# Layer 0 of the next pass is moved into layers 1 to 3 of this pass

## The chip, the cores and the metric

The kernel runs on one core of a Trainium2 chip. The metric is the device time of one execution in microseconds (us). A sample is an image of 128 channels by 32 by 32 pixels in float32; 16 samples go through the kernel in one execution.

## What is computed

Four residual layers run one after the other, each as `x = x + layer(group_norm(x))`, with 32 groups of 4 channels:

```
layer 0: offsets, mask = conv3x3(x -> 3 channels); bilinear sampling of x at the
         moved points, times the mask; depthwise 3x3; 1x1 (128 x 128)
layer 1: avg_pool3(x); conv3x3 -> 18 offsets + 9 masks; each of 9 taps is sampled
         bilinearly at its moved point; 3x3 convolution of the samples (128 x 128)
layer 2: conv3x3 (128 x 128) with weights made from weight and r_matrix
layer 3: 1x1 in; two directions (rows, then columns) of: depthwise 7-tap, 1x1 to 5
         kernels per head, tanh, weighted sum of 5 taps; two gates; 1x1 out
```

## The kernel before

One pass handles two samples, s = 0 and s = 1; eight passes make the 16. Seven of them are turns of a hardware loop (`one_pass(i, True)`), the last is written out (`one_pass(i, False)`). Channels lie on the 128 partitions, so an image is a tile of 128 x 1024. Each engine has its own program, written out by hand, and runs it in the order in which it is written; semaphores (`x_ready`, `n_blk` and so on) are all that ties the engines together. There is no scheduler.

In program order a pass of TensorE does this:

1. `near0` for both samples: the sampling of layer 0 in 8 tiles each. For a tile TensorE transposes two strips (L520) and two products of the hat functions (L526) and multiplies them (L535); VectorE makes the products (L1205) and copies the strips from PSUM (`block_copy`, L1116), ScalarE copies the transposed products (`G`) and at the end the sampled image `img`.
2. The depthwise convolution and the 1x1 of layer 0 in one: `w0[k]` is the 1x1 weight times tap k, and TensorE adds 4 (s = 0) or 7 (s = 1) taps (L644), while VectorE adds up the other 5 or 2 taps (`DW_TAPS`, L1223 to L1227), which go through one more matmul (L651). A tap is two matmuls, one for each half h of the image. VectorE then adds the residual (L1232), takes the statistics (`stats`, L1042 to L1046) and, with a small matmul for the mean over each group (`group_mean`) and a power on GpSimd, makes the scale and the bias of the normalisation (`affine`, L1054 to L1065); ScalarE applies them (`normalise`, L823); VectorE makes the 3x3 box sums (`pool3`, four instructions, L1177 to L1183).
3. Layer 1, s = 0: `offset_parts` (L456), `offsets` (L466), `doubles`, `far` (a count of offsets that reach too far; `load_flag` and a branch follow on each engine), `blocks` (transposes of the image, L551). VectorE makes the hat functions (L1315 to L1327), then in `near` the products (L1338) and transposes (L1349) of 8 tiles, with the box sums of s = 1 in between; TensorE samples (L580) and ScalarE copies.
4. The convolution `w1` of s = 0 (L482), with the offsets and blocks of s = 1 hooked in between its matmuls (`between`, a dictionary from (half, tap) to work); then `near` and `w1` of s = 1.
5. `w2` of both samples (layer 2), then the last residual, statistics and normalisation.
6. Layer 3: `P_X2`, `P_U`, `P_XC`, `P_MEAN`, the kernels of the first direction (`P_KERN`), those of the second, `P_GATE`, `P_OUT`. VectorE does the depthwise taps (L1402, L1407) and the weighted sums (L1421 to L1449) of each direction. Hooked in between the two directions are the layer 0 preparations of the next pass: normalisation (ScalarE), `start_parts` (twice `offset_parts`), `start_offsets`, `start_far`, and on VectorE `start_hats`.

The PSUM tensors are `psO[0]`, and `psN`, four banks of which `psO[1]` is the first two and `psT` the last two; `ps[0]` and `ps[1]` hold small results.

## Time and profile before

| | us |
|---|---|
| median of 3 runs | 2032.02 (2031.22 to 2033.98) |
| the profiled execution | 2024.91 |
| its span, first to last instruction | 2023.0 |
| TensorE busy | 1685.6 (83%) |
| VectorE busy | 1242.0 (61%) |
| ScalarE busy | 597.7 (30%) |
| mean granted TensorE clock | 0.911 of full speed |

The profile was taken from one execution, which was 7.1 us shorter than the median. PE is TensorE, DVE is VectorE, ACT is ScalarE, POOL is GpSimd, PEld the weight loads of TensorE. A float32 matmul of 512 columns stands in the trace as two records; a transpose as one. Busy time of TensorE is modelled and counts overlaps of neighbours, so that it is somewhat too high.

### The profile page before, as it was taken

How to read it: one execution, taken by the hardware profiler on the slowest of the kernel's cores; microseconds unless marked ns; L12 is line 12 of the kernel's file. 1: busy time of each engine (PE TensorE's matmuls, PEld its weight loads, DVE VectorE, ACT ScalarE, POOL GpSimd, SP SyncE). 2: the span in 40 equal slices, each digit the busy share in tenths (PEclk: the TensorE clock that was granted, in tenths of full speed). 3: DMA queues.
4: the chain of work that ended last, by engine and by line, in shares of the span. 5: the costliest groups of instructions: out<-in, count | busy, mean ns of one | idle time of the engine just before them, and what ended most of it. 6: DMA issues, size and time to landing. Idle time of an engine off the chain costs nothing.

```text
span 2023.0 us, 23653 instructions
## 1 busy us (share of the span) xinstructions
PE 1685.6 (83%) x7748; PEld 905.4 (45%) x7748; DVE 1242.0 (61%) x2281; ACT 597.7 (30%) x986; POOL 78.8 (4%) x92
## 2 busy tenths in 40 slices
PE   4979878898788987889878888879878798797984
PEld 3555344543445434554345533555335553355431
DVE  5655676546775387753877439664496654865546
ACT  2232422324324142230513305133141322313221
POOL 1000000000000000000001000010000000000000
PEclk8999989898889988899888998889989899897997
DMA  2000000000000000000000000000000000000000
GB/s 97 22 1 1 1 23 22 1 1 1 23 22 1 0 1 23 22 1 0 1 23 22 2 0 1 33 12 1 0 1 33 12 1 0 1 22 1 1 0 21
DMA packets 7108, 22.80 MB, mean 11 GB/s; under 512 B 1233, under 2 KB 1937, under 8 KB 6929
## 3 DMA queue, kind: packets, MB, share of 16 engines
q1 hardware_dynamic: 6928, 20.58, 2.8%
q8 instruction: 92, 1.51, 0.3%
q14 instruction: 88, 0.71, 0.1%
HBM read 12.19 MB, written 8.39 MB: 10 GB/s over the span
## 4 chain that ended last, share of the span: by engine, by line
issue 73%; DVE 12%; PE 11%; POOL 2%; ACT 1%; DVEq 0%; POOLq 0%
PE psO L456 2%; DVE GQt L1349 2%; PE psO L482 1%; DVE GTs L1338 1%; POOL gst L407 1%; DVE samp L1407 1%; DVE hf L1315 1%; DVE img L1183 1%; DVE hf L1320 1%; PE ps L466 1%; POOL strip L415 1%; PE psN L482 1%; ACT xn L823 1%; DVE hf L1327 1%; DVE pool_v L1179 1%
## 5 line engine op out<-in xcount | busy, mean ns | idle before, releaser
L482 PE MATMUL psO<-samp,w 128*128 128x512 f32 x576 | 259.4, 596 | 10.1 <-ACT samp L801 10.1
L580 PE MATMUL psN<-GQt,xq 64*128 64x144 f32 x2048 | 188.2, 334 | 89.6 <-DVE GQt L1349 71.8
L823 ACT ACTIVATE xn<-x,gst 128x1024 f32<-128x1024 f32 x48 | 60.2, 1254 | 536.8 <-DVE gst L1065 536.8
L580 PEld LDWEIGHTS psN<-GQt,xq 64*128 64x128 f32 x2048 | 161.3, 215 | 122.6 <-issue 57.5
L801 ACT ACTIVATE samp<-psN 128x576 f32<-128x576 f32 x256 | 155.9, 649 | 161.5 <-PE psN L580 161.2
L482 PEld LDWEIGHTS psO<-samp,w 128*128 128x128 f32 x576 | 105.0, 190 | 118.9 <-issue 118.9
L482 PE MATMUL psN<-xn,w 128*128 128x512 f32 x288 | 131.5, 605 | 0.0
L482 PE MATMUL psO<-xn,w 128*128 128x512 f32 x288 | 129.8, 603 | 0.0
L801 ACT ACTIVATE xq<-psN 128x512 f32<-128x512 f32 x144 | 81.6, 598 | 85.4 <-PE psN L551 80.0
L1338 DVE TENSOR_TENSOR GTs<-hf 128x576 f32<-128x576 f32 x128 | 104.1, 823 | 3.4
L801 ACT ACTIVATE G<-psN 120x256 f32<-120x256 f32 x128 | 49.1, 384 | 187.9 <-PE psN L526 186.8
L644 PE MATMUL psN<-img,w 128*128 128x512 f32 x224 | 101.6, 604 | 0.0
L407 POOL TENSOR_TENSOR gst<-gst,neg_half 128x1 f32<-128x1 f32 x64 | 35.0, 548 | 1621.7 <-DVE gst L1059 1621.6
L1349 DVE STREAM_TRANSPOSE GQt<-GTs 128x576 f32<-128x576 f32 x128 | 96.9, 766 | 0.0
L551 PE MATMUL psN<-ident,strip 128*128 128x128 f32 x512 | 87.0, 333 | 0.0
L1054 DVE COPY gst<-ps 128x2 f32<-128x2 f32 x64 | 10.1, 158 | 124.6 <-PE ps L447 124.6
L743 PE MATMUL psN<-samp,kv_w 128*128 128x512 f32 x96 | 60.3, 761 | 30.9 <-DVE samp L1407 30.9
L551 PEld LDWEIGHTS psN<-ident,strip 128*128 128x128 f32 x512 | 73.2, 175 | 28.2 <-issue 20.5
L1250 DVE TENSOR_TENSOR om<-ps,offb 128x216 f32<-128x216 f32 x16 | 6.1, 383 | 129.2 <-PE ps L466 129.2
L482 PEld LDWEIGHTS psO<-xn,w 128*128 128x128 f32 x288 | 53.5, 188 | 68.6 <-issue 68.6
L1116 DVE COPY xblk<-psN 120x256 f32<-120x256 f32 x128 | 54.3, 424 | 46.5 <-PE psN L520 46.5
L482 PEld LDWEIGHTS psN<-xn,w 128*128 128x128 f32 x288 | 53.0, 188 | 64.8 <-issue 64.8
(162 smaller groups left out, 2656.5 us busy)
## 6 DMA issues: line engine op xcount, KB each, us to landing
xin<-in_x SPq DMA_DIRECT2D x16, 512.0 KB, 3.4
out<-yout SPq DMA_DIRECT2D x16, 512.0 KB, 2.7
w<-in_w SPq DMA_DIRECT2D x2, 576.0 KB, 5.4
samp<-in_r SPq DMA_DIRECT2D x1, 576.0 KB, 6.7
tab<-in_tab SPq DMA_DIRECT2D x1, 494.0 KB, 5.0
kh_w<-in_kh SPq DMA_DIRECT2D x1, 320.0 KB, 5.8
kv_w<-in_kv SPq DMA_DIRECT2D x1, 320.0 KB, 5.9
woT<-in_woT SPq DMA_DIRECT2D x1, 256.0 KB, 6.5
```

The lines of the kernel that those rows point to most:

```text
L407: nc.gpsimd.tensor_tensor(out=g[:, 18:19], in0=g[:, 17:18], in1=neg_half[:], op=ALU.pow).then_inc(rstd_ready.sem, 1)
L456: last = mm(dst[32 * g:32 * g + 32, h, :], w[:, k, :], window(src)(h, k), start=(k < 4), stop=(k >= K9 - 4), skip_group_check=True)
L482: last = mm(dst[:, h, :], wgt[:, k, :], rhs(h, k), start=(k == 0), stop=(k == K9 - 1))
L551: last = nc.tensor.transpose(psT[:, t % 2, C * n:C * n + C], block, ident[:])
L580: last = mm(pair(u)[:, g, :].rearrange("p (k r c) -> p k r c", k=K9, c=SW)[:, :, :, cols], xQ[rows, t, a, e, :], w[rows, e, :, :, cols], s ...
L644: mm(psO[s][:, h, :], w0[:, k - min(DW_TAPS), :], window(img[s])(h, k), start=(k == DW_TAPS[s]), stop=False)
L743: mm(product(m), lhsT, rhs[:, HALF * h:HALF * h + HALF], start=True, stop=True)\
L801: return nc.scalar.activation(out, in_, ACT.Copy)
L823: nc.scalar.activation(inner(xn[s]), src[:].rearrange("p (r c) -> p r c", c=W), ACT.Identity, bias=g[:, 20:21], scale=g[:, 19:20]).then_in ...
L1116: v_.tensor_copy(xblk[b][:].rearrange("p h c -> p (h c)"), psT[0:BLK, 1, 0:2 * C])\
L1338: v_.tensor_tensor(GQ[n % 2][:].rearrange("p (k a b) -> p k a b", a=QR, b=QB), hy[:, n].unsqueeze(3).broadcast_to((C, PAIRS * K9, QR, QB)) ...
L1349: v_.transpose(GQt[o % RING][:].rearrange("p e k r c -> p (e k r c)"), GQ[(n - 1) % 2][:])\
```

## The change

The kernel becomes a pipeline over passes. What a pass of the loop does now, in the order of TensorE:

- It begins with the taps of layer 0 of its own sample 1 (`conv0(i, 1, ...)`, 18 matmuls, all nine taps on TensorE), put around `offset_parts`, `offsets`, `doubles` and `far` of sample 0. VectorE adds the residual and takes the statistics of sample 1 (`second_sample(0)`) after the hat functions of sample 0 and before its products; `affine` follows at tile 2, the box sums at tiles 4 to 7.
- The statistics and normalisation of the next two inputs (S0, S1; into `img`) stand behind the sampling of s = 0, with their `group_mean` hooked into `w1` of s = 0.
- `offset_parts`, `offsets` and the far count of the next pass are hooked into `w1` of s = 1; VectorE makes their offsets and hat functions ahead of the residual of `w1` of s = 1.
- `near0` of the next pass is hooked into `w2`: tiles of sample 0 into the second half of `w2` of s = 0, those of sample 1 into `w2` of s = 1. Both `w2` now write `psO[1]`. The residual of layer 2 goes to `yout`.
- The taps of layer 0 of the next sample 0 (`conv0(i + 1, 0, ...)`, `fill`) stand in pieces ahead of and inside layer 3, and `kernels(0)` ahead of `P_U`. Between the two directions VectorE adds its residual and takes its statistics, `affine` comes after the depthwise taps of the second direction, and the box sums in two pairs ahead of the weighted sums of the two halves. ScalarE's `normalise` for it stands ahead of the tanh of the second direction.
- VectorE's own taps (`DW_TAPS`, L1223 to L1227) and the matmuls behind them (L651) go. Ahead of the loop stand `near0` of both samples of pass 0 and the taps, residual, statistics and box sums of its sample 0.

```diff
 NEAR0, NEAR = 2.0, 1.0
 EARLY, LATE = 6, 9
-DW_TAPS = (5, 2)
-DVE_STEPS = 114
-START_STEPS = 29
+DVE_STEPS = 138
+START_STEPS = 38
 
...
-        POOL_AT = (2, 3, 4, 5)
+        POOL_AT = (4, 5, 6, 7)
...
+        P_X2 = 1
+        P_KERN = P_X2 + 2
+        P_U = P_KERN + 2 * TAPS
+        P_XC = P_U + 2
+        P_MEAN = P_XC + 2
+        P_GATE = P_MEAN + 2 + 2 * TAPS
         P_OUT = P_GATE + 2
+
+        def p_kern(v, h):
+
+            return (P_MEAN + 2 if v else P_KERN) + TAPS * h
+
...
+        EVENTS = ("L1B", "S0", "S1", "L2A", "L2B", "L3A", "L3B", "L1A")
+        LAST = ("L1B", "L2A", "L2B", "L3A", "L3B")
+        FIRST = ("S0", "S1", "L1A")
...
+        def norm_ends(name):
+
+            k = SAMPLE[name]
+            if name in ("S0", "S1"):
+                return xin[k], img[k]
+            return (yout if name in ("L3A", "L3B") else x)[k], xn[k]
...
@@ TensorE @@
+            def layer0(j, i=None):
+
+
+                def conv2(n, between={}, halves=(0, 1)):
+                    if i is None:
+                        return
+                    if n:
+
+                        pe.wait_ge(added.sem, added.at(i, 5))
+                        pe.wait_ge(xn_ready.sem, xn_ready.at(i, nth("L2B", EVENTS)))
+                    conv(psO[1], w2, window(xn[n]), between, halves)
...
+                        conv2(0, {(1, k): lambda k=k: near0(j, 0, k - 2) for k in range(2, K9)}, (1,))
+                        near0(j, 0, TILES - 1)
+
+                        pe.wait_ge(added.sem, added.at(i, 4))
+                        near0(j, 0, TILES)
+                        hooks = {(0, 2): third_mean}
+                        for n, hk in enumerate(((0, 3), (0, 5), (0, 7), (1, 0), (1, 2), (1, 4), (1, 6), (1, 8))):
+                            hooks[hk] = lambda n=n: near0(j, 1, n)
+                        conv2(1, hooks)
+                        near0(j, 1, TILES)
...
+            def conv0(j, s, first, last):
+
+
+                if first == 0:
+
+                    pe.wait_ge(img_ready.sem, img_ready.at(j, s + 1))
+                    if s:
+                        pe.wait_ge(added.sem, added.at(j, 1))
+                for n in range(first, last):
+                    h, k = n // K9, n % K9
+                    ins = mm(psT[:, h, :], w0[:, k, :], window(img[s])(h, k), start=(k == 0), stop=(k == K9 - 1))
+                if last == 2 * K9:
+                    ins.then_inc(conv_ready.sem, 1)
+
...
+                conv0(i, 1, 0, 7)
...
+                pe.wait_ge(y_ready.sem, y_ready.at(i, 0))
                 pe.wait_ge(pooled_ready.sem, pooled_ready.at(i, 1))
                 offset_parts(2, img[0], w1off)
...
+                conv0(i, 1, 7, 10)
                 offsets(i, 2, 27)
+                conv0(i, 1, 10, 12)
                 doubles(i, 0)
+                conv0(i, 1, 12, 14)
                 far(i, 2)
-                blocks(i, 0, range(2, TILES))
+                conv0(i, 1, 14, 18)
+                blocks(i, 0, range(TILES))
...
-                        near(i, s)
+                        near(i, s, lambda t, s=s: group_mean(i, "L1B", order) if s == 0 and t == 0 else None)
...
+                        hooks = {(0, 2): lambda: blocks(i, 1, (2, 3)),
+                                 (0, 4): lambda: (second_offsets(), blocks(i, 1, (4, 5))),
+                                 (0, 6): lambda: doubles(i, 1),
+                                 (1, 0): lambda: far(i, 3), (1, 2): lambda: blocks(i, 1, (6, 7))}
+                        if more:
+                            hooks[0, 1] = lambda: group_mean(i, "S0", order)
+                            hooks[0, 3] = lambda: group_mean(i, "S1", order)
+                        conv(psO[0], w1, samples, hooks)
                     else:
+                        hooks = {(0, 5): lambda: group_mean(i, "L2A", order)}
+                        if more:
+                            hooks[0, 2] = lambda: next_parts(0)
+                            hooks[0, 7] = lambda: next_parts(1)
+                            hooks[1, 0] = next_offsets
+                            hooks[1, 4] = lambda: offsets(i + 1, 1, 3)
+                            hooks[1, 8] = lambda: start_far(i + 1)
 
                         pe.wait_ge(added.sem, added.at(i, 3))
-                        conv(psO[0], w1, samples, {(0, 4): lambda: group_mean(i, 4)})
-
-
-                pe.wait_ge(xn_ready.sem, xn_ready.at(i, 5))
-                conv(psO[1], w2, window(xn[0]), {(0, 6): lambda: group_mean(i, 5),
-                                                 **({(1, 4): lambda: start_means(i + 1, False)} if more else {})})
-                pe.wait_ge(xn_ready.sem, xn_ready.at(i, 6))
-                conv(psO[0], w2, window(xn[1]), {(0, 6): lambda: group_mean(i, block3_norm(0, more))})
-
-                group_mean(i, block3_norm(1, more))
-
-                pe.wait_ge(xn_ready.sem, xn_ready.at(i, 8))
+                        conv(psO[0], w1, samples, hooks)
...
+                conv(psO[1], w2, window(xn[0]), halves=(0,))
+                group_mean(i, "L2B", order)
+                if more:
+                    layer0(i + 1, i)
+                else:
+                    conv(psO[1], w2, window(xn[0]), halves=(1,))
+
+                    pe.wait_ge(added.sem, added.at(i, 5))
+                    pe.wait_ge(xn_ready.sem, xn_ready.at(i, nth("L2B", order)))
+                    conv(psO[1], w2, window(xn[1]), {(0, 6): lambda: group_mean(i, "L3A", order)})
+
...
+                fill(0, 4)
+                group_mean(i, "L3B", order)
+                fill(4, 7)
...
+                fill(7, 14)
+                kernels(0)
...
+                fill(14, 16)
...
+                fill(16, 18)
...
+                    group_mean(i, "L1A", order)
+                kernels(1)
...
@@ ScalarE @@
+                    if s and more:
+                        normalise(i, "S0", order)
+                    if s:
+                        blocks(i, s, range(4))
...
+                            if s == 0 and u == 5:
+                                normalise(i, "L1B", order)
...
+                if more:
+                    normalise(i, "S1", order)
+                    parts(i + 1, 0)
+                    wide(i + 1, 0, i, order)
+                normalise(i, "L2A", order)
+                if more:
+                    parts(i + 1, 1)
+                    wide(i + 1, 1, i, order)
+                    start_masks(i + 1)
+                normalise(i, "L2B", order)
+                if more:
+                    layer0(i + 1)
+                normalise(i, "L3A", order)
+                normalise(i, "L3B", order)
+
...
+                    normalise(i, "L1A", order)
+                kernels(1)
...
@@ VectorE @@
+            def residual0(j, s):
+
+                dve.wait_ge(conv_ready.sem, conv_ready.at(j, s + 1))
+                v_.tensor_tensor(x[s][:], psT.rearrange("p b c -> p (b c)"), xin[s][:], ALU.add)\
+                    .then_inc(added.sem, 1)
+                dve.wait_ge(added.sem, added.at(j, s + 1))
+
+            def residual2(i, s):
+
+                dve.wait_ge(conv_ready.sem, conv_ready.at(i, 5 + s))
+                if s == 0:
+
+                    dve.wait_ge(yout_free.sem, yout_free.at(i, 0))
+                v_.scalar_tensor_tensor(yout[s][:], psO[1][:].rearrange("p b c -> p (b c)"),
+                                        vec[:, V_B2:V_B2 + 1], x[s][:], ALU.add, ALU.add).then_inc(added.sem, 1)
...
+                with dve.Else():
+                    for s in range(2):
+                        for n in range(TILES + 1):
+                            if n < TILES:
+                                product(TILES * s + n)
+                            if n == TILES and s == 0 and i is not None:
+
+                                residual2(i, 0)
+                            if n:
+                                block_copy(j, TILES * s + n - 1, (n - 1) % 2)
+                        if s == 0:
+                            third_stats()
+                    dve.wait_ge(n_blk.sem, n_blk.at(j, 2 * TILES))
...
+                def second_sample(part):
 
                     if part == 0:
+                        residual0(i, 1)
+                        stats(own, "L1B", order)
+                    elif part == 1:
+                        affine(own, "L1B", order)
                     else:
+                        pool3(own, 1, part - 2, i, order)
...
+                            if s == 0 and n == 2:
+                                second_sample(1)
                             if s == 0 and n in POOL_AT:
 
-                                pool3(1, POOL_AT.index(n))
+                                second_sample(2 + POOL_AT.index(n))
...
+                    if s == 0 and more:
+                        for k in range(2):
+                            start_stats(own, i + 1, k, order)
+                        for k in range(2):
+                            affine(own, ("S0", "S1")[k], order)
                 for s in range(2):
+                    if s and more:
+                        start_offsets(own, i + 1)
+                        for k in range(2):
+                            start_hats(own, i + 1, k)
 
...
+                    if v and more:
+                        residual0(i + 1, 0)
+                        stats(own, "L1A", order)
...
-                    if more and v == 1:
-                        start_offsets(nxt)
+                    if v and more:
+                        affine(own, "L1A", order)
                     for h in range(2):
+                        if v and more:
+                            for part in range(2 * h, 2 * h + 2):
+                                pool3(own, 0, part, i, order)
 
```

## Rows read from the trace of the kernel before

**Rows 1.** The page, part 1: busy time and instructions of the whole span.

```profile
PE 1685.6 (83%) x7748; PEld 905.4 (45%) x7748; DVE 1242.0 (61%) x2281; ACT 597.7 (30%) x986; POOL 78.8 (4%) x92
```

**Rows 2.** Windows of the second pass: length, busy (count) of each engine, PEclk, DMA.

```profile
285.70:332.40 46.70, 41.23 (x183) 25.38 (x182) 30.11 (x55) 9.56 (x21) 0.55 (x1) 0.96 0.08 27
332.40:352.90 20.50, 14.72 (x92) 9.70 (x93) 14.04 (x27) 7.09 (x13) 2.66 (x2) 0.81 0.09 27
352.90:371.60 18.70, 13.06 (x128) 11.41 (x129) 14.54 (x17) 9.97 (x16) 2.39 (x1) 0.77 0.00 1
371.60:401.30 29.70, 28.40 (x126) 14.51 (x126) 10.40 (x17) 5.62 (x12) 0.00 (x0) 0.93 0.01 1
401.30:414.50 13.20, 10.38 (x129) 8.68 (x129) 12.17 (x18) 9.54 (x16) 0.00 (x0) 1.00 0.01 2
414.50:469.80 55.30, 48.89 (x120) 21.68 (x120) 17.55 (x53) 5.02 (x4) 3.28 (x6) 0.98 0.00 0
469.80:534.80 65.00, 54.12 (x192) 21.26 (x192) 55.17 (x99) 27.49 (x41) 0.00 (x0) 0.86 0.02 7
```

**Rows 3.** Timeline of TensorE, second pass: start us, length us, work [idle before <-releaser].

```profile
288.44 0.43 PE L520 MATMUL psN<-ident,strip 128*120 128x128 f32 x2 [2.64 <-issue]
...
308.91 7.30 PE L644 MATMUL psO<-img,w 128*128 128x512 f32 x16 [0.58 <-PE psN L535]
...
332.42 4.61 PE L456 MATMUL psO<-img,w1off 128*32 128x512 f32 x36 [0.24 <-DVE img L1183]
...
380.81 1.04 PE L551 MATMUL psN<-ident,strip 128*128 128x128 f32 x8
381.69 1.88 PE L482 MATMUL psO<-samp,w 128*128 128x512 f32 x4
383.41 1.86 PE L466 MATMUL ps<-tab,Gd 128*128 128x27 f32 x16
...
469.82 3.68 PE L734 MATMUL psO<-xn,win2T 128*64 128x512 f32 x8 [3.12 <-ACT xn L823]
```

**Rows 4.** Timeline of VectorE, second pass: residual, statistics, box sums, affine.

```profile
317.96 1.22 DVE L1232 TENSOR_TENSOR x<-psO,xin 128x1024 f32<-128x1024 f32 x1 [2.38 <-PE psO L651]
...
321.13 0.22 DVE L1046 SCALAR_TENSOR_TENSOR gst<-gst 128x1 f32<-128x1 f32 x1 [0.27 <-DVE gst L1044]
...
327.23 1.29 DVE L1177 TENSOR_TENSOR pool_v<-xn 128x1088 f32<-128x1088 f32 x1 [1.33 <-ACT xn L823]
...
331.14 1.23 DVE L1183 TENSOR_TENSOR img<-img,pool_v 128x1024 f32<-128x1024 f32 x1
...
338.21 0.16 DVE L1054 COPY gst<-ps 128x2 f32<-128x2 f32 x1 [2.78 <-PE ps L447]
...
339.67 0.21 DVE L1065 TENSOR_SCALAR gst<-gst 128x1 f32<-128x1 f32 x1
```

**Rows 5.** Timeline of VectorE around the first sampling of layer 1.

```profile
343.98 2.16 DVE L1315 TENSOR_TENSOR hf<-tab,om 128x288 f32<-128x288 f32 x4 [0.71 <-DVE flag L1108]
...
350.65 1.43 DVE L1338 TENSOR_TENSOR GTs<-hf 128x576 f32<-128x576 f32 x2
...
366.05 1.42 DVE L1349 STREAM_TRANSPOSE GQt<-GTs 128x576 f32<-128x576 f32 x2
```

**Rows 6.** Timeline of ScalarE inside layer 3.

```profile
480.42 2.39 ACT L823 ACTIVATE xn<-xin,gst 128x1024 f32<-128x1024 f32 x2
482.69 1.25 ACT L984 ACTIVATE samp<-psO,vec 128x512 f32<-128x512 f32 x2
```

**Rows 7.** Timeline of VectorE inside layer 3.

```profile
483.98 0.69 DVE L1439 SCALAR_TENSOR_TENSOR samp<-x2p,samp 128x512 f32<-128x512 f32 x1 [1.01 <-ACT samp L984]
...
491.79 0.69 DVE L1439 SCALAR_TENSOR_TENSOR samp<-x2p,samp 128x512 f32<-128x512 f32 x1 [1.37 <-ACT samp L984]
...
522.64 0.15 DVE L1108 CAST flag<-ps 128x1 int32<-128x1 f32 x1
...
525.63 0.43 DVE L1079 SCALAR_TENSOR_TENSOR hat<-hat,mk 128x256 f32<-128x256 f32 x1
```

563 lines of the change are left out of this document (266 added, 297 removed).

## The prediction

> **What bounds the kernel now.** I began with the page's busy shares: TensorE is busy 83% of the span, VectorE 61% [rows 1]. That average says little, so the second thing read was the windows of one pass, the second, cut where TensorE's work changes: layer 0 (46.7 us), preparation of layer 1 (20.5), first sampling (18.7), `w1` of s = 0 (29.7), second sampling (13.2), `w1` of s = 1 with `w2` and the last normalisation (55.3), layer 3 (65.0); together 249.1 [rows 2]. The reader is to see three kinds of stage. In the fourth and the sixth TensorE is busy 28.4 of 29.7 and 48.9 of 55.3 us: matmuls set the time, and whatever is hooked in there is paid in full. In layer 3 VectorE is busy 55.2 of 65.0 us and TensorE's clock is at 0.86: VectorE sets the time, and TensorE's work there is cheap. In layer 0 and in the samplings the two take turns. Third came the timelines, for the price of each piece.
>
> **Prices.** A conv tap (one matmul of 512 columns): two take 383.41 - 381.69 = 1.72, so 0.86 us. Hooked work: 8 transposes between two taps start at 380.81 and the taps go on at 381.69, so 0.88, full price, nothing slips into their shadow. A tile of `near0` has 8 such short records: 0.9 when hooked (an estimate from that row); alone it costs (308.91 - 288.44)/16 = 1.28 with its start. `offset_parts` 4.6, `offsets` 1.9 [rows 3]. On VectorE residual and statistics 317.96 to 321.35 = 3.4, `affine` 338.21 to 339.88 = 1.7, box sums 327.23 to 332.37 = 5.1 [rows 4]; hat functions of layer 1 343.98 to 350.65 = 6.7, the 8 tiles 350.65 to 367.47 = 16.8 [rows 5]; `start_hats` of s = 0 522.64 to 526.06 = 3.4, of s = 1 about 3.1 (estimate, no flag to load) [rows 7]. One `normalise` on ScalarE 1.2 [rows 6].
>
> **Stage by stage, one loop pass after against before.**
>
> Layer 0, 46.7 before. It leaves the head of the pass: `near0` 20.5, TensorE's and VectorE's taps and the chain of residual, statistics and box sums. In its place stand the turn of the loop and 7 taps of sample 1, 6.0. The turn shows only as part of the 2.64 us of issue ahead of L520 [rows 3]; it lies between 0.7 and 2.7, I take 2.0, since the load of a flag is part of that row. Now 8.0, so -38.7. The wait for `yout` is covered by the taps.
>
> Preparation, 20.5 before. The chain is now parts 4.6, 3 taps 2.6, offsets 1.9, 2 taps 1.7, doubles 0.8 (by columns), 2 taps 1.7, far 0.3 = 13.6; 1.1 for flag and branch; hat functions 6.7; then residual and statistics of sample 1, 3.4, before the first product; 2.3 until the first tile reaches TensorE (350.65 against the window's edge at 352.9) [rows 2, 5]. Sum 27.1. TensorE's last 4 taps and 8 block tiles (3.4 + 7.2) end at 24.2, under it. So +6.6.
>
> First sampling, 18.7 before, paced by VectorE. `affine` adds 1.7 and waits some 0.4 for the mean, which stands behind tile 0. Then the box sums are late: ScalarE normalises only after the copy of the sixth step, which needs the third transpose; I count 2.1 us of wait at tile 4. That makes 4.2, of which about 1.3 comes back, as the last tiles are no longer queued up on TensorE behind VectorE: +2.9 (bounds 1.7 and 4.2).
>
> `w1` of s = 0, 29.7 before. ScalarE's program has `normalise(S0)` ahead of its block copies. It waits for the mean hooked at (0, 1): matmul, `affine` 1.7, normalise 1.2, one copy 0.6, some 3.8 in all, while TensorE does one tap and reaches block tile 2, which needs the first copy: a stall of 2.9, and 0.4 for two means. That ScalarE really holds later work back shows inside layer 3, where the tanh starts at 482.69, when two normalisations (480.42, 2.39) are through, and VectorE waits 1.01 and 1.37 for tanh [rows 6, 7]. +3.3. The Trainium skill says the same of the queues ("Perfetto Trace Analysis", section "Tensor Engine Instruction (MATMUL, LD_WEIGHTS)"): only TensorE may reorder a little, by pulling weight loads ahead, and the other engines are strictly first in, first out. This trace agrees by the 1.01 us; were it not so, the stall of 2.9 would be nothing and the pass 2.9 shorter.
>
> The other queues: GpSimd's strip copy for s = 1 now stands ahead of the power of S0; both engines' work there is small (2.66 us of GpSimd in the whole preparation window [rows 2]) and the mean of S0 comes some 12 us after the box sums. SP's loads of the next input are issued as before, when the residual has read the old one: for sample 0 already in layer 3, for sample 1 some 18 us ahead of its statistics. Both at 0; a load that is late would hold S1's statistics and with them the hooked offsets.
>
> Second sampling: as before, 0.
>
> `w1` of s = 1 and `w2`, 55.3 before. Taps of `w1` 15.8 with its mean, and hooked in: parts of both next samples 9.2, offsets 3.7, far 0.4: 29.1. Before, these 13.3 us lay in layer 3 under VectorE. Then half of `w2` 7.7, to 36.8. VectorE meanwhile gets the far count at 28.2, makes both hat functions (3.4 + 3.1), and only then residual and statistics: 38.1, mean 38.4; TensorE waits 1.6. Flag and branch 1.0 (between 0.7 and 1.3): 39.4. Second half with the first 7 tiles: 7.7 + 0.45 + 6 x 0.9 = 13.6, to 53.0. Tile 7, and the last product waits for `residual2` (1.3) and a strip copy that stands behind it on VectorE: 2.4, to 55.4. `w2` of s = 1 with mean and 8 tiles: 15.5 + 0.2 + 6.8 = 22.5, to 77.9; last product and end of the branch 0.8, 78.7. The last chain (`affine` of sample 0, residual, statistics, mean, `affine`, normalise: 1.7 + 3.4 + 0.2 + 1.7 + 1.2 and waits) takes until 86.3; the 7 taps of `fill` stand in it for nothing (if the chain were shorter they would cost up to 6.0). So +31.0.
>
> Layer 3, 65.0 before, paced by VectorE. TensorE comes warm: `P_X2` takes 3.68 for 8 records now, after a wait [rows 3], in a window with the clock far below 1, so -1.0 for its first half. The two waits for tanh go: -2.4. `start_offsets` goes: -1.0. The cast and hats stood in the shadow of the gate's matmul: 0. Between the directions 3.4 more, the 18th tap being done in time to within 0.2 us (4 taps more would cost 3.4). Behind the taps of direction two `affine` 1.7 and a wait of 1.4 for normalise; tanh waits behind it, and is ready before VectorE has done two box sums. Box sums 5.1. Sum +7.2. The 11 taps of `fill` in here (9.5 us) are hidden by VectorE.
>
> On the clock the rows say: 0.77 in the first sampling, 0.81 in the preparation, 1.00 in the second sampling [rows 2], so it falls where TensorE waits between short pieces; of its two levels, 1.2 and 2.4 GHz, the lower is then granted part of the time. The Trainium skill ("TensorE: Matmul & The Clock Gate", section "What's actually happening") has it that the low rate is the default and activity lifts it. By the rows the first matmuls after the first sampling stay slow in both kernels and nothing changes; by the rule read generously the fill would keep layer 3 at full rate and the gate's two matmuls would save some 2 us a pass.
>
> **The sum.** -38.7 + 6.6 + 2.9 + 3.3 + 0 + 31.0 + 7.2 = +12.3 us for a pass of the loop, 7 times = +86. Ahead of the loop: `near0` 20.5, a wait for the sampled image 1.3, 18 taps 15.5, then 3.4 + 0.2 + 1.7 + 1.2 + 5.1 = 11.6 before the box sums are there; before, from the start of `near0` to `parts` it was 332.42 - 288.44 = 44.0 [rows 3]: +5. The last pass has no next one: +6.6 + 2.9 + 1.4 (second `w2` waits for `residual2`, as both use `psO[1]`) - 1 = +10. Total +101. Against the profiled execution's 2024.9 that is 2126; the median is 7.1 above that execution, so 2032 + 101 = 2133.
>
> **The rivals.**
> (a) The hooked short work is free: transposes and small matmuls run in the shadow of the 512-column taps and their weight loads. Tiles 13.1 and offsets 3.7 would then cost nothing, 16.8 a pass: 12.3 - 16.8 = -4.5, 7 times = -32, with +15 outside: 2015, faster. It decides only if a hooked record costs under a seventh of its price (101 of 118 us must go). For it: the weight loads overlap in the page (905 us of PEld beside 1686 of PE) [rows 1]. Against it: 0.88 for 8 transposes between taps [rows 3].
> (b) VectorE's extra work in layer 3 finds room, since 65.0 - 55.2 = 9.8 us there are idle [rows 2]. Then +5.1 a pass, 36 + 15: 2083. Against it: most of that idle time is at the gate and the output, where the new work does not stand.
> (c) The small waits of each hook are not hidden: a tile costs its 1.28 as it does alone. 15 tiles x 0.4 = 6 a pass: 2133 + 42 = 2175. For it: three engines hand over at every tile. Against it: a tap of 0.86 lies between two tiles, about the length of product and copy.
> (d) It is milder, as TensorE stays warm where its windows now show 0.86 and 0.93 [rows 2]: at the lower level a matmul takes twice its time, and 2 us each at the gate, and at the head of `w1` of s = 0, would go: 4 us a pass less, 2105. For it: `fill` leaves fewer gaps. Against it: none of the fill stands next to either place.
>
> **Numbers.** Forecast 60%, (a) 8%, (b) 8%, (c) 12%, (d) 12%. Predicted 2133. To leave out no more than two in ten the range runs from just under (b) to just over (c): 2075 to 2180; the likeliest case's own range is 2110 to 2155 (the bounds of turn, branch, sampling and tile). A difference under 0.2% (4 us) can't be told from none. Faster comes from (a) alone, near its end, and so does no change: faster 0.06, same 0.03, slower 0.91.
>
> **What the next profile would show.** Right: passes some 12 us longer; `parts` of layer 1 some 8 us behind the last matmul of the pass before; TensorE idle about 3 us ahead of the second pair of block tiles in `w1`; 2 us of wait of VectorE for normalise at tile 4; the stretch from the end of the second sampling to `P_X2` about 86 us; layer 3 about 72 us. Wrong: hooked tiles well under 0.9 us, a layer 3 that stays at 65, or waits at each hook. The prediction fails on the side of the sign only if the sixth stage grows by under 17 us instead of 31 (101/7 = 14 less).

## The result, and the profile after

| | before | after |
|---|---|---|
| median, runs taken side by side | 2033.00 us (2031.22 to 2034.58, 4 runs) | 2153.70 us (2151.84 to 2155.79, 4 runs) |
| profiled execution, span | 2024.91, 2023.0 us | 2155.79, 2154.0 us |
| granted TensorE clock | 0.911 | 0.904 |

The ratio is 1.0594 (95% interval 1.0576 to 1.0613): 120.7 us slower, where 101 were forecast. The side was right, and the time lies inside the range. It lies as near to rival (c), 2175, as to the forecast, 2133, so that the total alone could not tell the two apart; the rows below can.

Page of the changed kernel, part 1, for [rows 1]:

```profile
PE 1745.8 (81%) x7908; PEld 928.1 (43%) x7908; DVE 1182.8 (55%) x2227; ACT 600.8 (28%) x986; POOL 79.1 (4%) x92
```

VectorE lost 59 us of work, TensorE gained 60, and the kernel gained 131 us of span. The sum of the work hardly moved; it is the places that changed.

Windows of the second pass after, for [rows 2] (length, busy of each engine, PEclk, DMA). The first is the head with the taps of sample 1; the other six are the stages of the forecast in its order:

```profile
350.60:356.80 6.20, 6.20 (x15) 2.40 (x13) 1.28 (x1) 0.00 (x0) 0.00 (x0) 1.00 0.28 114
356.80:383.75 26.95, 21.57 (x114) 11.38 (x113) 13.20 (x22) 5.86 (x12) 0.00 (x0) 0.94 0.11 39
383.75:405.97 22.22, 15.70 (x130) 13.76 (x131) 17.37 (x28) 11.11 (x17) 2.65 (x2) 0.69 0.00 0
405.97:437.10 31.13, 27.20 (x132) 14.52 (x132) 12.74 (x29) 6.86 (x13) 1.10 (x2) 1.00 0.01 1
437.10:450.24 13.14, 10.35 (x129) 8.64 (x129) 12.06 (x18) 9.54 (x16) 0.00 (x0) 1.00 0.00 1
450.24:536.66 86.42, 83.07 (x367) 43.48 (x367) 31.06 (x89) 20.22 (x33) 2.19 (x4) 1.00 0.00 1
536.66:613.38 76.72, 51.18 (x109) 20.18 (x110) 58.96 (x91) 20.96 (x32) 3.02 (x2) 0.80 0.02 6
```

| stage of the second pass | before | forecast | after |
|---|---|---|---|
| layer 0, or head | 46.7 | 8.0 | 6.2 |
| preparation | 20.5 | 27.1 | 26.9 |
| first sampling | 18.7 | 21.6 | 22.2 |
| `w1` of s = 0 | 29.7 | 33.0 | 31.1 |
| second sampling | 13.2 | 13.2 | 13.1 |
| `w1` of s = 1, `w2`, last chain | 55.3 | 86.3 | 86.4 |
| layer 3 | 65.0 | 72.2 | 76.7 |
| sum | 249.1 | 261.4 | 262.8 |

The only stage that is off by more than 2 us is layer 3. TensorE at its start in the second pass, after (timeline; start us, length us, idle before and its releaser in brackets), and at the end of layer 3 in the first pass:

```profile
536.66 2.00 PE L817 MATMUL psO<-xn,win2T 128*64 128x512 f32 x8 [0.37 <-ACT xn L915]
```

```profile
334.74 3.78 PE L821 MATMUL psO<-xc,xq 128*128 128x512 f32 x4 [14.39 <-DVE xq L1590]
340.80 2.07 PE L861 MATMUL psO<-samp,woT 128*128 128x512 f32 x2 [2.29 <-DVE xq L1600]
342.66 1.91 PE L862 MATMUL psO<-at,xq 128*128 128x512 f32 x2
344.37 1.91 PE L861 MATMUL psO<-samp,woT 128*128 128x512 f32 x2
...
349.70 1.02 PE L862 MATMUL psN<-at,xq 128*128 128x512 f32 x2
350.56 6.32 PE L686 MATMUL psN<-img,w 128*128 128x512 f32 x14
```

And the gate and the first output pair in the second pass of before:

```profile
521.72 3.77 PE L743 MATMUL psO<-xc,xq 128*128 128x512 f32 x4 [5.94 <-DVE xq L1461]
...
527.80 1.12 PE L776 MATMUL psO<-samp,woT 128*128 128x512 f32 x2 [2.31 <-DVE xq L1473]
```

Four things are to be seen. `P_X2` comes warm, 2.00 us where [rows 3] have 3.68. Ahead of the gate TensorE now stands idle for 14.39 us, where it was 5.94. The output matmuls behind it run at 1.91 to 2.07 us a pair, half the rate of the 1.02 at the end: of the two levels the lower, 1.2 GHz, is granted. And the turn of the loop, for which 2.0 us were set, shows no gap: the taps (350.56) start when the last output pair has.

VectorE, and then GpSimd, between the two halves of the second direction, first pass:

```profile
325.79 0.85 DVE L1555 TENSOR_TENSOR GTs<-ahp 128x672 f32<-128x672 f32 x1
326.56 2.59 DVE L1568 SCALAR_TENSOR_TENSOR samp<-ahp,samp 128x512 f32<-128x512 f32 x1
329.07 0.68 DVE L1568 SCALAR_TENSOR_TENSOR at<-GTs,samp 128x512 f32<-128x512 f32 x1
```

```profile
326.13 2.47 POOL L428 COPY strip<-img 128x2304 f32<-128x2304 f32 x1 [13.55 <-DVE img L1271]
```

One instruction of 0.68 us takes 2.59: its record ends at 329.15, 0.55 us behind the end of GpSimd's copy of the strips (326.13 + 2.47 = 328.60). It is so in all seven passes of the loop. The copy was always there; before, it ran elsewhere (from 332.62 in the second pass, at the head of the preparation). It starts when the box sums are done, and the box sums now end in the middle of VectorE's busiest stretch. The Trainium skill ("SBUF — State Buffer", section "Who interferes with whom") has the rule: a VectorE instruction with two inputs in SBUF and a GpSimd instruction that reads SBUF exclude each other, and the later one waits for the whole of the other. The trace agrees: `ahp` and `samp` are both in SBUF, and behind the copy's end the instruction needs 0.55 us more, about what it takes alone. The copy, too, takes 2.47 where it takes 2.10 at 401.90: it started while the sum of 325.79, with both inputs in `ahp`, was still running. e1 below tests it.

**Only one pass of before was read.** `offset_parts` of s = 1, in three passes of before:

```profile
371.63 6.61 PE L456 MATMUL psN<-img,w1off 128*32 128x512 f32 x36 [1.30 <-ACT samp L801]
620.23 4.59 PE L456 MATMUL psN<-img,w1off 128*32 128x512 f32 x36 [1.30 <-ACT samp L801]
868.66 4.59 PE L456 MATMUL psN<-img,w1off 128*32 128x512 f32 x36 [1.14 <-ACT samp L801]
```

The second pass, which all stages of the forecast were taken from, had these matmuls slow; of the other seven only the last had (6.38), the rest 4.59. So the 29.7 us of that stage were 2 too long as a base. The other passes differ too: 246.0 to 246.4 us for four of the seven, 249.1 for the second, and 248.6 for the third and the fifth, whose `offset_parts` take 4.59 but whose output runs partly at half rate. Over the whole loop, from the first to the last `offset_parts` of s = 0, before and after:

```profile
86.10 4.61 PE L456 MATMUL psO<-img,w1off 128*32 128x512 f32 x36 [0.25 <-DVE img L1183]
1817.43 4.61 PE L456 MATMUL psO<-img,w1off 128*32 128x512 f32 x36 [0.25 <-DVE img L1183]
```

```profile
93.67 4.63 PE L463 MATMUL psO<-img,w1off 128*32 128x512 f32 x36
1937.00 4.63 PE L463 MATMUL psO<-img,w1off 128*32 128x512 f32 x36
```

(1817.43 - 86.10)/7 = 247.3 us a pass before, and (1937.00 - 93.67)/7 = 263.3 after: +16.0, seven times +112. Ahead of the loop it is +7.6 (forecast +5), and from the last `offset_parts` to the end 205.6 against 217.0, +11.4 (forecast +10). Together 131.0, the whole difference of the spans.

### The profile page after: what moved, and what is told of

Same layout as the page of the kernel before. It is cut to its first block, busy times and chain, and to the rows that moved or that the text cites. A ratio compares the mean times of both kernels' runs of the same rounds, so it can differ in the third digit from the quotient of the medians.

```text
span 2154.0 us, 23860 instructions
## 1 busy us (share of the span) xinstructions
PE 1745.8 (81%) x7908; PEld 928.1 (43%) x7908; DVE 1182.8 (55%) x2227; ACT 600.8 (28%) x986; POOL 79.1 (4%) x92
## 4 chain that ended last, share of the span: by engine, by line
issue 80%; DVE 8%; PE 6%; POOL 3%; ACT 1%; POOLq 0%; DVEq 0%; ACTq 0%
POOL gst L420 2%; POOL strip L428 1%; DVE GQt L1462 1%; PE psO L489 1%; DVE GTs L1451 1%; PE psN L489 1%; ACT xn L915 1%; DVE at L1578 1%; DVE img L1271 1%; PE psN L593 1%; PE psO L821 1%; PE psN L686 1%; DVE samp L1533 1%; DVE pool_v L1265 1%; DVE img L1269 0%
## 5 line engine op out<-in xcount | busy, mean ns | idle before, releaser
L593 PE MATMUL psN<-GQt,xq 64*128 64x144 f32 x2048 | 209.0, 358 | 101.5 <-DVE GQt L1462 86.4
L489 PE MATMUL psN<-xn,w 128*128 128x512 f32 x576 | 278.8, 607 | 5.9 <-issue 4.6
L686 PE MATMUL psN<-img,w 128*128 128x512 f32 x576 | 273.5, 616 | 4.5 <-PE psO L547 4.5
L593 PEld LDWEIGHTS psN<-GQt,xq 64*128 64x128 f32 x2048 | 178.2, 237 | 134.7 <-issue 80.6
L686 PEld LDWEIGHTS psN<-img,w 128*128 128x128 f32 x576 | 105.2, 190 | 140.2 <-issue 140.2
L489 PEld LDWEIGHTS psN<-xn,w 128*128 128x128 f32 x576 | 99.1, 190 | 87.8 <-issue 85.6
L821 PE MATMUL psO<-xc,xq 128*128 128x512 f32 x32 | 30.0, 1094 | 106.9 <-DVE xq L1590 106.9
L915 ACT ACTIVATE xn<-x,gst 128x1024 f32<-128x1024 f32 x32 | 40.3, 1258 | 250.3 <-DVE gst L1162 250.3
L1058 ACT ACTIVATE samp<-psN,vec 128x512 f32<-128x512 f32 x96 | 64.4, 687 | 76.3 <-PE psN L821 76.3
L547 PE MATMUL psO<-G,xblk 120*128 120x128 f32 x512 | 79.7, 278 | 6.9 <-DVE xblk L1213 6.7
```

The source lines that it names most:

```text
L489: last = mm(dst[:, h, :], wgt[:, k, :], rhs(h, k), start=(k == 0), stop=(k == K9 - 1))
L547: last = mm(psO[0][:, p // 4, C * (p % 4):C * (p % 4) + C], xblk[p % 2][:, u, :], G1[p % 2][:, u, :], start=(u == 0), stop=(u == 1))
L593: last = mm(pair(u)[:, g, :].rearrange("p (k r c) -> p k r c", k=K9, c=SW)[:, :, :, cols], xQ[rows, t, a, e, :], w[rows, e, :, :, cols], s ...
L686: ins = mm(psT[:, h, :], w0[:, k, :], window(img[s])(h, k), start=(k == 0), stop=(k == K9 - 1))
L821: mm(product(m), lhsT, rhs[:, HALF * h:HALF * h + HALF], start=True, stop=True)\
L915: nc.scalar.activation(inner(dst), src[:].rearrange("p (r c) -> p r c", c=W), ACT.Identity, bias=g[:, 20:21], scale=g[:, 19:20]).then_inc( ...
```

## The experiments

Each was timed in 3 rounds beside the kernel before (median 2033.0 to 2033.5). "A pass" is the mean distance of the seven passes of the loop in the profiled execution, as above; 263.3 in the changed kernel, 247.3 in the kernel before. The last column is against the changed kernel's 2153.7.

| kernel | median us | ratio to before | a pass | to the change |
|---|---|---|---|---|
| changed kernel | 2153.70 | 1.0594 [1.0576, 1.0613] | 263.3 | |
| e1_strip_late | 2147.28 | 1.0555 [1.0522, 1.0588] | 262.1 | -6.4 |
| e2_s0_late | 2128.05 | 1.0466 [1.0435, 1.0497] | 259.4 | -25.7 |
| e3_taps_at_gate | 2127.83 | 1.0466 [1.0436, 1.0495] | 259.4 | -25.9 |
| e7_first_sampling | 2123.11 | 1.0444 [1.0426, 1.0461] | 259.6 | -30.6 |
| e10_box_sums_last | 2090.56 | 1.0275 [1.0242, 1.0308] | 254.4 | -63.1 |
| e4_end_of_l3 | 2063.73 | 1.0153 [1.0123, 1.0182] | 250.6 | -90.0 |
| e8_three | 2003.32 | 0.9859 [0.9842, 0.9875] | 242.6 | -150.4 |
| e9_two_taps | 1988.16 | 0.9769 [0.9736, 0.9803] | 240.5 | -165.5 |
| e5_parts_after | 2145.77 | 1.0554 [1.0536, 1.0571] | 263.0 | -7.9 |
| e6_parts_before | 2046.80 | 1.0066 [1.0049, 1.0083] | 251.8 | |

**e4_end_of_l3.** All of VectorE's new work in layer 3 goes to where VectorE waits: residual and statistics behind the last sum ahead of the gate, `affine` and box sums behind the last product ahead of the output. TensorE's `group_mean` and ScalarE's `normalise` follow.

```diff
-                    if v and more:
-                        residual0(i + 1, 0)
-                        stats(own, "L1A", order)
...
                     .then_inc(l3_csum.sem, 1)
+                if more:
+                    residual0(i + 1, 0)
+                    stats(own, "L1A", order)
...
                 v_.tensor_scalar(wo2, woT[:, :, 1, :], st3[:, 2:3], None, ALU.mult).then_inc(l3_maps.sem, 1)
+                if more:
+                    affine(own, "L1A", order)
+                    for part in range(4):
+                        pool3(own, 0, part, i, order)
```

> The changed kernel, with residual and statistics of the next sample 0 moved from between the two directions of layer 3 to VectorE's wait for the gate, and its affine step and box sums to the wait for the output matmuls. Theory A, VectorE's chain sets layer 3 and these 12 us or so stood on it: 3.4 + 0.7 of wait, 1.7 + 1.3, 5.1, 1.9 of the long instruction and up to 2.7 of slow output matmuls come off, about 14 a pass, less 1 to 3 as the outputs are made later: 7 x 11 to 13, 2063 to 2077. Theory B, the extra work in layer 3 was mostly covered (TensorE or ScalarE set it): under 4 us a pass, 2126 or more.

90 us less, 12.7 a pass, as theory A has it. TensorE in e4:

```profile
320.21 3.77 PE L821 MATMUL psO<-xc,xq 128*128 128x512 f32 x4 [6.27 <-DVE xq L1582]
326.27 1.12 PE L861 MATMUL psO<-samp,woT 128*128 128x512 f32 x2 [1.40 <-DVE xq L1595]
```

Counted from the first `offset_parts` (90.64 here, 93.67 in the changed kernel) the gate comes 11.5 us earlier (229.6 instead of 241.1), the wait ahead of it is 6.27 instead of 14.39, and in this pass the output runs at the full rate, 2.8 us less (so do the third, fifth and seventh; in the others it starts at 1.32 to 2.07 a pair). So the loss of the change is for three quarters a loss of place in layer 3.

**e10_box_sums_last.** Only `affine`, `normalise` and the box sums are moved as in e4; residual and statistics stay between the directions.

```diff
-                    if v and more:
-                        affine(own, "L1A", order)
                     for h in range(2):
-                        if v and more:
-                            for part in range(2 * h, 2 * h + 2):
-                                pool3(own, 0, part, i, order)
...
                 v_.tensor_scalar(wo2, woT[:, :, 1, :], st3[:, 2:3], None, ALU.mult).then_inc(l3_maps.sem, 1)
+                if more:
+                    affine(own, "L1A", order)
+                    for part in range(4):
+                        pool3(own, 0, part, i, order)
```

> The changed kernel with only the affine and the box sums of the next pass's sample 0 moved from the second direction of layer 3 to behind the last VectorE work ahead of the output (and ScalarE's normalisation behind its last sigmoid); residual and statistics stay between the two directions, where they cost 3.4 us of VectorE by the rows. e4_end_of_l3 moved all of it and gave -90 us, 12.9 a pass. Theory A (in layer 3 VectorE's time is paid in full, instruction by instruction): e10 keeps the 3.4 us, so it gives 12.9 - 3.4 = 9.5 a pass, -66 us: 2088; the gate wait of TensorE (14.4 us) falls to some 4 to 5 us and the output matmuls run at full rate (7.0 instead of 9.8). Theory B (the residual and the statistics lie in a wait that VectorE has there anyway, and the whole loss is the box sums, the wait for the normalisation and the copy on GpSimd): e10 gives as much as e4, -90 us: 2064.

Theory A: 2091 where it said 2088. The two parts of e4 are 8.9 us a pass for the box sums and what goes with them, and 3.8 for residual and statistics (254.4 - 250.6), whose instructions are 3.4. So VectorE's new work in layer 3 is paid, and finds no room there. The 8.9 are not its instructions alone: they hold the wait for `normalise`, the 1.9 us of the long instruction and a share of the output's rate. The forecast of the output failed in part: the gate's wait is 6.62 instead of 4 to 5, and in the first pass the output pairs take 1.37, 1.91 and 1.66, not 1.02.

**e1_strip_late.** GpSimd's strip copy for s = 0 also waits until VectorE has written the first `yout`.

```diff
-                wait_apart(pool, (pooled_ready, pooled_ready.at(i, s + 1)), (q_blkp, q_blkp.at(i, TILES * s)))
+                wait_apart(pool, (pooled_ready, pooled_ready.at(i, s + 1)), (q_blkp, q_blkp.at(i, TILES * s)),
+                           *([(y_ready, y_ready.at(i, 0))] if s == 0 else []))
```

> The changed kernel, with GpSimd's strip copy of sample 0 held back until the outputs of the pass before are made. In the changed kernel one weighted-sum instruction of VectorE in layer 3 takes 2.59 us instead of 0.68 while GpSimd's copy (2.47 us) runs. Theory A, the two engines get in each other's way: the long instruction falls to about 0.68, layer 3 gets 1.9 us shorter in each of 7 passes, 2153.7 - 13 = 2140. Theory B, the long instruction has another cause (its place in the program): it stays at 2.6 and the time at 2154.

The same instruction in e1, and the copy:

```profile
326.73 0.68 DVE L1569 SCALAR_TENSOR_TENSOR samp<-ahp,samp 128x512 f32<-128x512 f32 x1
```

```profile
349.27 2.10 POOL L429 COPY strip<-img 128x2304 f32<-128x2304 f32 x1 [36.52 <-DVE yout L1605]
```

The row answers the question of the mechanism: without the copy beside it, it takes 0.68 us, and the wait of TensorE at the gate falls from 14.39 to 12.49 in each of the seven passes. But 7 x 1.9 = 13 us should have come, and 6.4 did. In e1 the first two passes are 260 us long and the five after them 262.8, as in the changed kernel. In the third pass:

```profile
673.87 1.60 PE L565 MATMUL psN<-ident,strip 128*128 128x128 f32 x8 [2.55 <-ACT xq L894]
675.26 1.91 PE L490 MATMUL psO<-samp,w 128*128 128x512 f32 x2
```

Behind the stall for `normalise(S0)` the matmuls now run at half rate (1.91 for a pair), where the changed kernel has 1.02 in the same place in its first five passes (1.82 and 1.92 in the sixth and seventh). From `offset_parts` of s = 1 to `P_X2` it is 130.7 us in the first pass of e1, as in the first four of the changed kernel, and 133.3 to 133.5 in its last five: 2.7 us lost by the rate, where 1.9 were gained at the gate and 1.2 at the output. So theory A has the mechanism, and the time lies midway between A and B.

**e2_s0_late.** ScalarE copies the block tiles of `w1` before it normalises S0.

```diff
                     if s:
                         blocks(i, s, range(4))
+                    if s and more:
+                        normalise(i, "S0", order)
```

(the two lines stood ahead of `blocks`.)

> The changed kernel, with ScalarE's normalisation of S0 placed behind its first four block copies instead of ahead of them. Theory A, the wait of 2.56 us of TensorE ahead of block tile 2 is the order of ScalarE's program: it goes, 7 x 2.6 = 18 us less, 2136. Theory B, the copies were not what held TensorE, or the wait comes back at the next hook (offsets wait for S1): 2150 to 2154.

TensorE in the changed kernel, then in e2, at the second pair of block tiles:

```profile
416.10 1.14 PE L564 MATMUL psN<-ident,strip 128*128 128x128 f32 x8 [2.56 <-ACT xq L893]
```

```profile
408.94 1.04 PE L564 MATMUL psN<-ident,strip 128*128 128x128 f32 x8
```

The stall of 2.56 (forecast 2.9) is gone with the order alone, so it was ScalarE's program order. The yield, 4.0 us a pass and 26 us in all where theory A had 18, is more than the stall; part of the rest is rate: the third and fourth output pairs of the first pass take 1.02 each in e2, 1.91 and 1.21 in the changed kernel.

**e7_first_sampling.** The mean of sample 1 ahead of the tiles, not behind tile 0, and ScalarE normalises two tiles earlier.

```diff
-                        near(i, s, lambda t, s=s: group_mean(i, "L1B", order) if s == 0 and t == 0 else None)
+                        if s == 0:
+                            group_mean(i, "L1B", order)
+                        near(i, s)
...
-                            if s == 0 and u == 5:
+                            if s == 0 and u == 3:
                                 normalise(i, "L1B", order)
```

> The changed kernel, with the group mean of L1B ahead of the first tile instead of behind it, and ScalarE's normalisation behind the fourth copy instead of the sixth. VectorE waits 1.5 us for the one and 1.8 us for the other in the first sampling. Theory A, VectorE's order of work paces this stage: both waits go, 8 x 3.3 = 26 us less, 2127. Theory B, TensorE at half its clock (0.69 in this window, 2.3 us for a tile) paces it: 0 to 1 us a pass, 2146 or more.

VectorE waited for this mean and this normalisation in the changed kernel:

```profile
386.59 0.16 DVE L1150 COPY gst<-ps 128x2 f32<-128x2 f32 x1 [1.51 <-PE ps L454]
...
392.91 1.29 DVE L1265 TENSOR_TENSOR pool_v<-xn 128x1088 f32<-128x1088 f32 x1 [1.82 <-ACT xn L915]
```

In e7 the second wait is 0.51 and the first is gone; 3.7 us a pass, where theory A had 3.3. The change had two waits there that are nothing but order. The forecast had 0.4 for the first, and 2.1 for the second.

**e3_taps_at_gate.** The seven taps of sample 1 go from the head of the pass to ahead of the gate, into TensorE's 14.4 us.

```diff
-                conv0(i, 1, 0, 7)
...
                 kernels(1)
+                if more:
+                    conv0(i + 1, 1, 0, 7)
```

> The changed kernel, with the 7 taps of sample 1 that open a pass moved to the wait ahead of the gate of the pass before, where TensorE stands idle for 14.4 us. Theory A: the taps are hidden there and leave the head of the pass, where the next work must then wait only for the outputs, some 2.5 us after the last matmul: 6.2 - 2.5 = 3.7 us less a pass; and with TensorE idle for only about 8 us ahead of the gate the output matmuls (9.8 us against 7.0 in the kernel before) run at full rate sooner, up to 2.7 less: in all 7 x 3.7 to 6.4, 2109 to 2128. Theory B, the clock has nothing to do with that idle time: output matmuls stay at 9.8, 2128.

-25.9 us, 3.9 a pass of the 6.2 that the head took, which is theory B to the microsecond (2128): `offset_parts` now waits 1.46 for `yout`, which the taps had covered. The output stays at half rate although TensorE has had 6.3 us of taps at the full rate 8.2 us earlier:

```profile
335.18 3.77 PE L820 MATMUL psO<-xc,xq 128*128 128x512 f32 x4 [8.23 <-DVE xq L1592]
341.24 2.07 PE L862 MATMUL psO<-samp,woT 128*128 128x512 f32 x2 [2.29 <-DVE xq L1602]
```

**e8_three.** The edits of e4, e2 and e7 together.

> Three edits in one: work of the next sample 0 at the end of layer 3, S0 normalised behind the block copies, and the first sampling with the earlier mean and normalisation. If each cost stands by itself on the chain: 2063.7 - 25.6 - (what the sampling edit alone gives, up to 26) = 2012 to 2038. If the second and the third only uncover other waits: 2050 to 2064.

The gains add up: 12.7 + 4.0 + 3.7 = 20.4 a pass, and 20.7 are there. The time is 9 us under the lower end of the forecast, since the sampling edit alone gave 30.6 us and not at most 26. This version is 1.4% faster than the kernel before as it stood. So the move of layer 0 need not cost anything; what made the change a loss is where its short work was put. Whether the kernel before would gain as much from such reordering was not run.

**e9_two_taps.** e8 with two of the seven head taps put between the small mean and the output.

```diff
                 if more:
                     group_mean(i, "L1A", order)
+                    conv0(i + 1, 1, 0, 2)
...
-                conv0(i, 1, 0, 7)
+                conv0(i, 1, 2, 7)
```

> The kernel of e8_three with the first two of the seven head taps of sample 1 moved into the gap between the small mean matmul at the gate (317.04) and the first output matmul (318.97), where TensorE is idle some 1.3 us and where e8 then gives the first three output matmuls at half rate (2.07, 1.91, 1.90 us for a pair of records instead of 1.02 to 1.12). Theory A (what matters for the rate is how long TensorE was idle just before; fill the gap and the output runs at full rate, as in e4_end_of_l3): the output shrinks from 9.6 to about 7.0 us, the two taps go from 0.9 us each at the head into the gap: -0.9 to -2.6 from the taps and -2.6 from the rate, less 1.0 of taps that push the output back, so -3 us a pass, 7 times = -21: about 1982 us. Theory B (the rate at the output is set by the longer wait of 6.3 us ahead of the gate, and two taps do not lift it): the taps run at half rate themselves, 1.9 to 3.7 us, push the output by up to 1.5 us and give back 1.8 at the head: between -5 and +10 us in all, about 2003.

```profile
315.80 3.66 PE L823 MATMUL psO<-xc,xq 128*128 128x512 f32 x4 [6.62 <-DVE xq L1586]
319.93 0.38 PE L454 MATMUL ps<-gst,tab 128*128 128x2 f32 x2 [0.47 <-DVE gst L1145]
320.17 2.00 PE L686 MATMUL psN<-img,w 128*128 128x512 f32 x4
322.02 1.02 PE L864 MATMUL psO<-samp,woT 128*128 128x512 f32 x2
```

15 us under e8, between A (21) and B (none), and nearer to A; in this pass the two taps run at the full rate (2.00 for their four records) and the output pairs take 1.02 from the first one on. In three of the seven passes the first pair takes 1.37 to 1.38, in the others all take 1.02. 2.3% faster than the kernel before, 7.7% faster than the changed one.

**e5_parts_after and e6_parts_before.** `offset_parts` of layer 0 adds 4 of its 9 taps, in the changed kernel and in the kernel before: part of the offset convolution is left out, so that this work costs half.

```diff
+                taps_used = K9 if n >= 2 else 4
                 for h in range(2):
-                    for k in range(K9):
+                    for k in range(taps_used):
```

> The changed kernel with part of the work left out: the offset convolution of layer 0 uses 4 of its 9 taps (8 matmuls for a sample instead of 18). 4.6 us of offset_parts for a sample become about 2.0, 5.1 us for a pass. Theory A: hooked into w1 of s = 1, TensorE's work is paid in full, 7 x 5.1 = 36 us less (and 3 to 5 ahead of the loop), about 2114. Theory B, the hooked matmuls are partly covered, since VectorE's hat functions and the wait for their statistics end the stretch: under half of that, 2135 or more.

> The same work left out of the kernel before, where these matmuls lie in layer 3 under VectorE. Theory A: nearly nothing to be had there beyond the 3 to 5 us ahead of the loop and a little of the 2.4 us a pass for which VectorE waits for tanh: 2033 down to 2015. Theory B, TensorE sets layer 3 in the kernel before: 36 us less, 1997.

In e6 less work of TensorE inside layer 3 made the kernel 13.8 us slower (0.66%, clock 0.880 to 0.885 where the kernel before had 0.906 to 0.910 beside it); both theories had it faster. The output of its second pass:

```profile
526.44 2.07 PE L777 MATMUL psO<-samp,woT 128*128 128x512 f32 x2 [2.30 <-DVE xq L1474]
```

2.07 where the kernel before has 1.12 in that pass (527.80). It is so in all seven passes, and `offset_parts` of s = 1 take 6.51 to 6.56 from the second pass to the seventh, 4.59 before in all of these but one. So this work cost nothing in layer 3, as the forecast had it, and with part of it left out the granted clock is lower. In e5 each of the two parts of a pass shrinks from 4.63 to 1.99, 37 us over seven passes, and only 8 come back, 6.2 of them ahead of the loop. The sixth stage of the second pass, from the start of `w1` of s = 1 to the branch ahead of the second half of `w2`, in the changed kernel and in e5:

```profile
450.24 1.98 PE L489 MATMUL psO<-samp,w 128*128 128x512 f32 x4 [1.28 <-ACT samp L893]
...
488.40 0.38 PE L454 MATMUL ps<-gst,tab 128*128 128x2 f32 x2 [0.77 <-DVE gst L1141]
489.45 2.03 PE L489 MATMUL psN<-xn,w 128*128 128x512 f32 x4 [0.66 <-issue]
```

```profile
446.19 1.98 PE L490 MATMUL psO<-samp,w 128*128 128x512 f32 x4 [1.28 <-ACT samp L894]
...
479.06 0.38 PE L454 MATMUL ps<-gst,tab 128*128 128x2 f32 x2 [0.77 <-DVE gst L1142]
483.04 3.68 PE L490 MATMUL psN<-xn,w 128*128 128x512 f32 x4 [3.59 <-issue]
```

Up to the small mean it is 38.16 us against 32.87: the 5.3 us are saved in full where the hooked parts stand, as theory A has it. Then the wait at the branch takes 3.59 instead of 0.66, and the four records behind it run at half rate, 3.68 instead of 2.03: 4.6 of the 5.3 are gone. The releaser is "issue", so no engine is named. One thing differs in the DMA rows: a 16 KB load of instructions (queue 8) starts inside this wait in each of the seven passes of e5, and none starts inside it in any of the changed kernel. That points to a wait for instructions, but no run tested it.

## Why the forecast was right, and where it was short

**The sixth stage, +31.0: right.** 86.4 against 86.3. A hooked tile costs 0.88 us of TensorE (492.63 to the taps at 493.51), forecast 0.9:

```profile
492.63 0.38 PE L529 MATMUL psN<-ident,strip 128*120 128x128 f32 x2
492.85 0.38 PE L535 MATMUL psN<-ident,GT 128*120 128x128 f32 x2
493.06 0.61 PE L547 MATMUL psO<-G,xblk 120*128 120x128 f32 x4
493.51 1.05 PE L489 MATMUL psN<-xn,w 128*128 128x512 f32 x2
```

That ends rival (a) (free in the shadow) and rival (c) (1.28 each, waits at every hook): the rows carry no wait. The forecast's milestones hold as well, counted from 450.24: the second half of `w2` begins behind the branch at 39.2 (forecast 39.4), tile 7 is through at 55.5 (55.4), the last tap of `w2` ends at 78.2 (77.9). The last chain is luck in part: the terms that the forecast gives for it, from 78.7, come to 86.9 without a wait, not 86.3; in the trace its `affine` begins at 77.6 already (527.85), and that makes up for waits of 0.66 (twice, for GpSimd) and 0.92 (for the mean).

**The first three stages: right to within 2 us each.** The head is 1.8 shorter, as the loop's turn was priced at 2.0 and costs TensorE nothing. The first sampling is 0.6 longer: the wait for the mean was set at 0.4 and is 1.51, the wait at tile 4 at 2.1 and is 1.82. e7 shows that both are order.

**`w1` of s = 0, +3.3: the mechanism right, the base wrong.** The stall came (2.56) and e2 removes it. Yet the stage grew only by 1.4 in this pass, as its `offset_parts` had taken 6.61 in the pass that was read, and takes 4.60 now. In six of the eight passes of before it takes 4.59 anyway, so there the stall counts in full. This is the first part of the shortfall: the second pass of before is 249.1 us long, the mean pass 247.3, 1.8 x 7 = 12 us over the loop. The step that failed is that one pass stood for all seven. Against the medians it weighs less, since the profiled execution of before was itself 8 us faster than its median: if these 8 us are spread over the eight passes (an estimate from 2033.0 - 2024.9), about 5 of the 12 are left.

**Layer 3, +7.2: the mis-sized term.** It measured +11.7. The instructions were counted rightly: residual and statistics take 3.2 us in the second pass, `affine` 1.7, the wait for `normalise` 1.32, the box sums 5.1. Rival (b), that they find room, is dead by e4 and e10.

```profile
561.49 1.22 DVE L1276 TENSOR_TENSOR x<-psN,xin 128x1024 f32<-128x1024 f32 x1 [0.66 <-PE psN L686]
...
577.15 1.29 DVE L1265 TENSOR_TENSOR pool_v<-xn 128x1088 f32<-128x1088 f32 x1 [1.32 <-ACT xn L915]
```

What was missing: 1.9 us for the VectorE instruction that waits for GpSimd's copy, and 2.8 us for the output at half rate (603.61 to 613.38, 9.8, against 527.80 to 534.80, 7.0). The wait of the residual for its 18th tap, set at 0, is 0.66; `P_X2` gives 1.7 and not 1.0, which evens that out. The forecast had priced GpSimd's copy for s = 1 alone, at 0, and did not ask what starts the one for s = 0. Its passage on the clock priced nothing at the output; in the second pass it is the largest term that is missing. By the groups of instructions over all eight passes, the output's matmuls into `psO` sum to 53.3 us after and 40.6 before, so that on the mean it is 1.6 a pass.

**The clock, rival (d).** `w1` of s = 0 now begins at the full rate in all eight passes (`offset_parts` 4.59 to 4.60), but before it did so in six of the eight as well, so that the 2 us of the rival were to be had in two passes only. The gate does not come at the full rate: 3.4 to 3.8 us for four records in every kernel shown. And the output got slower, which is the other way.

**The sum.** On the profiled executions 131 against 101. The 30 us are: 12 from the pass that was read, 10 from the stages of that pass (13.7 instead of 12.3 a pass), 4 since the mean pass after (263.3) is longer than its second one, 2.6 ahead of the loop, and 1.4 in the last pass. On the medians it is 120.7, since the profiled execution of before was 8 us under its median and that of after 2 above. That the sum came so near is luck in part: layer 3 was 4.5 us a pass too low, and the head and `w1` of s = 0, 1.8 and 1.9 too high, hid most of it.

## What to carry to other kernels

When work is moved, move it to where its engine waits, not only to where the other engine is busy: with the residual and the box sums in VectorE's waits ahead of gate and output, +5.9% became +1.5% (e4), and with two changes of order and two taps in a gap of TensorE -2.3% (e9). Read the stages of several passes before one stands for all, and ask of each moved step what it releases on engines that look idle. Price a stall together with the rate of the matmuls behind it, and look at the rate in several passes.

## What the runs showed of the hardware

- GpSimd is busy 4% of the span and still cost VectorE 1.9 us a pass: an instruction with two inputs in SBUF went from 0.68 to 2.59 us beside a copy of 2.1 to 2.5 us. In e8 the same copy runs from 327.12 to 329.22 beside the second addition to `yout` (328.76), one of whose tensors is in PSUM, and that one keeps its 1.28 us.
- The length of the last wait doesn't alone decide the rate behind it. e4 and e8 have the same code at the gate and the same 6.27 us of wait ahead of it in the first pass; the first output pair takes 1.12 in e4 (its row stands above) and 2.07 in e8:

```profile
318.97 2.07 PE L863 MATMUL psO<-samp,woT 128*128 128x512 f32 x2 [1.34 <-DVE xq L1597]
```

- A gain can be lost to this, as in e1 (13 us of row, 6 of time), or grow by it, as in e2 (18 us of stall, 26 of time).
- Less work can be slower: e6, 0.66%, with the output and `offset_parts` of s = 1 at half rate or partly so in nearly every pass.
- The turn of the hardware loop left no gap on TensorE (349.70, then 350.56). No run took the turn away.
